# Eight weight loads of an attention and mixture-of-experts kernel, moved on SyncE's queue from batches 4 to 12 of attention into batches 12 to 15

## The reference

```python
x = x + attention(layernorm(x), ctx_512, ctx_512)
x = x + moe(layernorm(x), gate_w, w1, w2, w3)

# attention: 16 batches, 128 queries and 128 keys, 32 query heads on 8 key heads, head size 8
scores = einsum('bkgsd,bktd->bkgst', q, k) / sqrt(8)
out = einsum('bkgst,bktd->bkgsd', softmax(scores), v)

# moe: 2048 tokens of 256, 8 experts of width 512, the best 2 of each token
probs = softmax(einsum('ti,ei->te', xt, gate_w))
weights, indices = top_k(probs, 2); weights = weights / weights.sum(-1)
x1 = silu(einsum('ti,eoi->teo', xt, w1)); x3 = einsum('ti,eoi->teo', xt, w3)
out = sum over the two experts of weights * einsum('teo,eio->tei', x1 * x3, w2)
```

## Time and profile before

| | us |
|---|---|
| median of 3 timed runs | 450.33 |
| lowest, highest | 449.58, 451.56 |
| the profiled execution | 449.8 |
| its span | 448.0 |
| mean granted clock of TensorE in it | 0.92 |

### The profile page before, as it was taken

One profiled execution on the slowest core, in us unless ns is written; L12 is line 12 of the kernel. 1 busy time (PEld: TensorE's weight loads), 2 busy tenths in 40 slices (PEclk: granted clock), 3 DMA queues, 4 the chain that ended last, 5 costly groups with the idle time before them and its releaser, 6 DMA issues.

```text
span 448.0 us, 8599 instructions
## 1 busy us (share of the span) xinstructions
PE 363.3 (81%) x2234; PEld 259.2 (58%) x2256; DVE 234.7 (52%) x659; ACT 197.6 (44%) x397; POOL 183.8 (41%) x361
## 2 busy tenths in 40 slices
PE   0177988888789889873139999999999999999991
PEld 0045444455445444322127888888888888888870
DVE  6776796888678857656962332322232322232320
ACT  3325777776567646787313222223222223222220
POOL 6661363377646534576411222233222233222232
PEclk9997999999799979885559999999999999999997
DMA  6676888988977785331420333333333333333222
GB/s 197 153 150 110 228 230 200 256 192 250 221 231 169 173 243 164 107 121 50 174 72 25 51 58 49 58 48 47 48 57 48 55 51 47 47 56 50 35 23 23
DMA packets 46209, 51.16 MB, mean 114 GB/s; under 512 B 18659, under 2 KB 39267, under 8 KB 46179
## 3 DMA queue, kind: packets, MB, share of 16 engines
q1 hardware_dynamic: 37299, 39.64, 34.9%
q0 software_dynamic: 7152, 9.34, 13.2%
q10 hardware_dynamic: 1728, 1.82, 1.3%
HBM read 31.51 MB, written 16.69 MB: 108 GB/s over the span
## 4 chain that ended last, share of the span: by engine, by line
PE 58%; DMA 13%; DVE 10%; POOL 6%; issue 6%; SPq 4%; ACT 2%; POOLq 0%; ACTq 0%
PE bank L898 25%; PE bank L916 15%; DMA qst<-negT 10%; PE bank L908 4%; DVE wlo L1306 3%; PE bank L720 3%; PE bank L733 3%; PE bank L697 3%; PE bank L694 2%; PE bank L886 2%; DMA qparts_d<-qp 2%; POOL slots_d L545 2%; SPq L315 1%; SPq L282 1%; PE bank L773 1%
## 5 line engine op out<-in xcount | busy, mean ns | idle before, releaser
L660 POOL DMA_INDIRECT out_rows<-ys,meta x39 | 60.9, 1561 | 155.5 <-DVE ys L1537 149.3
L1251 DVE TENSOR_REDUCE negm<-bank 128x4 f32<-128x512 f32 x128 | 84.3, 682 | 27.6 <-PE bank L697 23.9
L1530 DVE TENSOR_TENSOR gat<-bank,sil 128x512 f32<-128x512 f32 x39 | 27.0, 692 | 112.5 <-PE bank L898 112.5
L967 ACT ACTIVATE prob<-bank 128x512 f32<-128x512 f32 x128 | 73.0, 596 | 27.4 <-PE bank L720 22.0
L916 PE MATMUL bank<-w,gT 128*128 x312 | 73.9, 380 | 0.8 <-ACT gT L1171 0.8
L1165 ACT ACTIVATE sil<-bank 128x512 f32<-128x512 f32 x39 | 23.3, 598 | 105.8 <-PE bank L898 105.8
L898 PE MATMUL bank<-whi,xhi 128*128 x156 | 60.3, 468 | 1.2 <-ACT xhi L1159 1.2
L916 PEld LDWEIGHTS bank<-w,gT 128*128 128x128 f32 x312 | 56.3, 190 | 7.1 <-issue 1.0
L697 PEld LDWEIGHTS bank<-kst,qst 125*128 125x128 bf16 x512 | 42.2, 103 | 25.0 <-issue 5.4
L720 PE MATMUL bank<-qst,kst 128*128 128x512 bf16 x107 | 43.2, 409 | 13.5 <-DMA qst<-negT 11.5
L697 PE MATMUL bank<-kst,qst 125*128 125x128 bf16 x512 | 52.6, 229 | 0.5 <-issue 0.2
(11 more groups left out here) (121 smaller groups left out, 479.3 us busy)
## 6 DMA issues: line engine op xcount, KB each, us to landing
xs<-slots_d SPq DMA_DIRECT2D x39, 129.0 KB, 2.0
w<-in_w1T SPq DMA_DIRECT2D x8, 512.0 KB
w<-in_w3T SPq DMA_DIRECT2D x8, 512.0 KB
w<-in_w2T SPq DMA_DIRECT2D x8, 512.0 KB
qparts_d<-qp SPq DMA_DIRECT2D x16, 192.0 KB, 4.4
qst<-qparts_d SPq DMA_DIRECT2D x16, 192.0 KB
qst<-qparts_d SPq DMA_DIRECT2D x16, 128.0 KB
vblk<-in_v SPq DMA_DIRECT2D x16, 128.0 KB
```

The lines of the kernel that those rows point to most:

```text
L660: pool.indirect_dma_start(out, IndirectOffsetOnAxis(ap=meta[:, r4, 0:1].bitcast(I32), axis=0), ys[:, r4, :], None, compute_op=ALU.add).the ...
L967: act.activation(prob[:, k, :], ps_e[k % 2][:, :], ACT.Exp, scale=SCALE).then_inc(exp_done, 1)
L1251: dve.tensor_reduce(negm[:, b % 2, g * G:(g + 1) * G], ps_s[(8 * b + g) % 3][:, :].rearrange("p (h t) -> p h t", h=G), AX.X, ALU.max, nega ...
L1530: dve.tensor_tensor(gat[:, u, :], ps_h3[u][:, :], sil, ALU.mult).then_inc(g_done, 1)
```

## The change

The eight calls of load_w2 on SyncE's queue move. Before, they stand in turns 4, 5, 6, 8, 8, 10, 11 and 12 of the loop; after, in turns 12, 13, 13, 14, 14, 15, 15 and 15. Nothing else is changed. The instructions of TensorE, VectorE, ScalarE and POOL are the same, in the same order.

```diff
--- before.py
+++ after.py
@@ -367,6 +367,12 @@
             load_x(12)
             load_x(15)
             for i in range(-2, B):
+                if i == 13:
+                    load_w2(1)
+                if i == 14:
+                    load_w2(3)
+                if i == 15:
+                    load_w2(5)
                 if i == 7:
                     load_w13(11)
                 if i % 2 == 0 and 2 <= i + 3 < B:
@@ -377,10 +383,6 @@
                     store_x2(i - 2)
                 if i % 2 == 1 and 0 <= i + 1 < B:
                     lay_neg(i + 1)
-                if i == 8:
-                    load_w2(3)
-                if i == 11:
-                    load_w2(6)
                 if i % 2 == 0 and 0 <= i + 1 < B:
                     lay_neg(i + 1)
                 if i % 2 == 1 and 3 <= i + 4 < B:
@@ -399,12 +401,6 @@
                     load_v(i + 1)
                 if i == 3:
                     load_w13(6)
-                if i == 4:
-                    load_w2(0)
-                if i == 5:
-                    load_w2(1)
-                if i == 8:
-                    load_w2(4)
                 if i == 2:
                     load_w13(4)
                 if i % 2 == 1 and 0 <= i + 1 < B:
@@ -417,10 +413,16 @@
                     load_w13(1)
                 if i % 2 == 0 and 8 <= i + 1 < B:
                     load_res(i + 1)
+                if i == 12:
+                    load_w2(0)
+                if i == 13:
+                    load_w2(2)
+                if i == 14:
+                    load_w2(4)
+                if i == 15:
+                    load_w2(6)
                 if i == 3:
                     load_w13(7)
-                if i == 10:
-                    load_w2(5)
                 if i % 2 == 0 and 0 <= i - 4 < B - 2:
                     copy_rows((i - 4) // 2)
                 if i % 2 == 1 and 2 <= i + 4 < B:
@@ -435,13 +437,11 @@
                     load_w13(3)
                 if i % 2 == 0 and 2 <= i + 4 < B:
                     load_k(i + 4)
-                if i == 6:
-                    load_w2(2)
                 if i % 2 == 1 and 0 <= i - 1 < B:
                     store_x2(i - 1)
                 if i == 2:
                     load_w13(5)
-                if i == 12:
+                if i == 15:
                     load_w2(7)
                 if i == 8:
                     load_w13(13)
```

## The result

Over 18 timed runs each, the kernel before took 449.94 us (median) and the changed kernel 444.74. The ratio is 0.9895, with a 95% interval of 0.9871 to 0.9919, so the change makes the kernel 1.05% faster. Forecast were 445.3 us, in a range of 440.5 to 452. The profiled execution of the changed kernel took 443.68 us, with a span of 441.8 us and a mean granted clock of 0.943, where before had 448.0 and 0.92. One profile is one execution: the timed runs of before spread from 446.1 to 454.1 us and those of after from 442.1 to 450.3, as wide as the effect. The ratios and their intervals leave out the executions that ran over 1.5% above a kernel's fastest at a lower granted clock, while a median in us is over all timed ones.

The account below looks back on a forecast made before the run. Attention's end sets when the expert tiles start, and DMA is crowded within attention. Terms -2.6 (waits), -3.3 (clock) and +0.9 (last four batches) sum to -5.0 us, from 450.33 to 445.3 us, range 440.5 to 452.

Parts of the forecast that it names:

- term A: Crowded middle of attention: TensorE's waits for lay_neg at batches 6, 8, 10 and 12 shrink, -2.6 us (0 to 5.3 gained).
- term B: Middle of attention: one of two 6.8 us stretches with TensorE's clock at 0.50 goes, -3.3 us (0 to 6.6 gained).
- What bounds the kernel: Attention's end decides when expert tiles start; in attention DMA is crowded, 0.85 busy from 80.3 to 166.1 us.
- What a load costs: Middle of attention: each 512 KB load takes all 16 engines 1.9 us; seven give back 13.6 us, share 0.85 to 0.69.
- Term C: Last four batches: moved loads delay lay_neg(15) and perhaps other small transfers, +0.9 us (0 to 3.4).
- the first: Batch 14, in Term C: lay_neg(14), with two loads ahead instead of one, still lands within its 5.67 us cover.
- The third: Batch 15, in Term C: copy_rows(5), with w2(4) in front, lands at 194.0 us, before POOL's scatter wants it at 194.92.
- The waits stay: Middle of attention: other transfers keep the queue full, lay_neg still lands in 6 us, nothing gained; 450.2 us, chance 0.24.
- Everything goes well: Whole attention stage: wait and clock gains come in full, late batches cost nothing; 440.5 us, chance 0.08.
- The slower one: Last batches decide: lay_neg(14) and (15) land in 7.32 us, TensorE waits 5.1 us, clock may fall; 452.8 us, chance 0.15.

Follow-up runs that it names:

- e11: Kernel before, its seven w2 loads still in the middle (turns 4 to 10) but each right behind a lay_neg; 449.33 us, ratio 1.007.
- e12: Kernel before, plus seven w2 pieces loaded a second time at the changed kernel's places in batches 12 to 15; 452.37 us, ratio 0.999.
- e1: Changed kernel with all eight w2 loads issued behind the last copy_rows, after batch 15; 447.93 us, ratio 0.994.
- e2: Changed kernel with w2(0), (1), (4) and (7) issued behind copy_rows(4), (5) and (6) instead of ahead; 444.62 us, ratio 0.988.
- e9: Changed kernel with the late w2 loads put where the trace of before shows the DMA engines idle; 441.94 us, ratio 0.981.
- e7: Changed kernel with lay_neg issued by ScalarE on its own DMA queue instead of by SyncE; 455.5 us, ratio 1.014.
- e3: Kernel before plus five dummy TensorE products ahead of each lay_neg wait from batch 1 on, no transfer moved; 450.12 us, ratio 1.003.
- e5: Kernel before with w2(3) to (6) moved to turns 14 and 15, the other w2 loads left in place; 451.0 us, ratio 1.003.
- e6: Kernel before with w2(0), (1), (2) moved to turns 12 and 13, the other w2 loads left in place; 446.93 us, ratio 0.997.
- e4: Changed kernel plus five dummy TensorE products ahead of each lay_neg wait from batch 1 on; 442.32 us, ratio 0.984.
- e10: e9 plus five dummy TensorE products ahead of each lay_neg wait from batch 1 on; 443.1 us, ratio 0.986.

## Why the prediction was right, and which of its steps were not

**The sum.** Forecast -5.0 us, measured -5.2 by the medians. That it came so close is in part luck: in this pair of profiles term A brought nothing and term B more than its value, and the two misses made up for each other. In the profiles the middle, batch 5 to 13, went from 85.9 to 79.9 us, -6.0, where terms A and B together said -5.9; the rest came in ahead of the first moved load (lay_neg(5) at 78.89 instead of 80.28, the same instructions, so chance) and went again in the last batches.

**What bounds the kernel.** Right. Attention sets when the tiles start, and these keep 217.2 us behind the same 13.59 us of waiting for split_lo.

**What a load costs.** Too high. Between the issues of lay_neg(5) and lay_neg(13) the busy time of the 16 engines went from 0.85 x 85.8 = 72.9 us to 0.77 x 79.87 = 61.5. That is 11.4 us for seven loads, 1.6 us each and not 1.9. The forecast share of 0.69 also left the stretch at its old length, though it was to get shorter.

**Term A, the waits (-2.6).** In this pair of profiles its step failed. Batches 6, 8, 10 and 12 waited 0, 1.70, 1.19 and 0.27 us, 3.2 instead of 5.26, which looks like -2.1. But batches 5, 9 and 13 wait more than before, and the sum over batches 5 to 13 rose from 7.7 to 9.4 us. The landings did not shrink: lay_neg(8) took 8.03 us against 7.32 in the earlier trace rows, and lay_neg(10) 6.55 against 6.46 on the chain of before. Over all profiles a smaller gain may be there: the waits of batches 5 to 13 are 7.7, 11.8 and 10.5 us in before, e11 and e12, and 9.4, 6.6, 8.3 and 8.5 in the changed kernel, e1, e2 and e9, in the mean 1.8 us less, with ranges that overlap. The reasoning from loads that stand ahead of lay_neg in SyncE's queue falls with e11 (loads behind it cost as much) and e7 (another queue lands no sooner). Shown is that batches 5 to 13 take 85.9, 86.7 and 87.4 us with seven loads in that stretch and 79.3 to 81.8 us with none and lay_neg on SyncE: 86.7 against 80.6 in the mean, 6.1 us.

**Term B, the clock (-3.3, one of two stretches).** Right in kind, too small in size, and sharper than foreseen in its place. The two stretches of 6.8 us at 0.50 are gone, and one of 3.4 us behind batch 13 has come: 10.2 us less at the lower clock, worth 5.1 us by the prediction's own way of counting. Over all profiles one place stands out, from lay_neg(8) to lay_neg(9): 14.7 to 16.1 us in all six kernels that have w2(0) to (2), or all seven loads, in turns 4 to 10, and 11.3 to 12.4 us in all eight others. Part of it is clock. From the first product of batch 8 to lay_neg(9) before took 124.73 - 117.36 = 7.4 us and after 119.83 - 115.54 = 4.3, the same work at 0.50 and at 1.00. How much of the total comes by the clock is not settled. Half of the time at 0.50 is 6.5 us in the mean of before, e11 and e12, and 0.9 in that of the four without loads, so by this count 5.6 of the 6.1 us in the middle are clock. With dummies, seven loads cost 84.0 us against the mean of 80.0 and 80.4, 3.8 us, of which e3's remaining stretch at 0.50 is 1.7; so 2.1 us are left that are not clock. In the timed runs the mean clock differs by 0.007, which over 448 us is 6.3 us at the lower level, or 3.1 us of the 5.2. These three estimates put the clock at 0.6 to 0.9 of the gain, where the forecast had 3.3 of 5.9. Against them stand e3's timed runs, which reached the changed kernel's clock and won nothing, as far as the dummies' own time doesn't hide a gain.

**Term C, the last four batches (+0.9).** The size fits the profile of the changed kernel (65.9 us instead of 64.8, +1.1) and lies between the nothing and the 2 us that e12 and the other profiles leave; the timed runs of e12 can neither confirm nor exclude it. Of its steps the first held: lay_neg(14) was covered, and lay_neg(15), issued at 178.84, cost TensorE 0.35 us. The third was called harmless and was the one that counted: copy_rows(5) was forecast to land in 4.8 us, ahead of the scatter that wanted it. It took 4.42 at the least, until POOL's own work was done, and its scatter came 1.6 us late, which fits a later landing, though the trace names no cause for that wait. copy_rows(4), which I had not costed, took 6.24 us, but made its scatter only 0.3 us late. I had taken the scatter's place in the profile of before as its due time; counted from the copy's issue, POOL's own work ended 5.1 us behind it before (194.10 + 0.22 against 189.24) and 4.4 us in the changed kernel.

**The rivals.** "The waits stay" was right about the waits and wrong about the time. "Everything goes well" had -11.9 us; three quarters of its clock part came (5.1 of 6.6), its waits did not. The slower one did not come: lay_neg(15), issued at 178.84, let TensorE go on at 182.10, 3.3 us later and not 7.3.

**What stays open.** By which wait the traffic of the middle costs the part that is not clock isn't settled. The waits for lay_neg don't show it in this pair. VectorE's waits for TensorE's scores fell from 11.5 to 8.7 us and ScalarE's for the exp products from 13.0 to 9.1, but these are waits for TensorE itself. Open too is why batch 8, and nothing else, splits so cleanly. Its waits for lay_neg are 1.98 to 3.31 us in the six kernels and at most 1.70 in the eight, but a wait of 2.28 us at batch 5 of the changed kernel had no low clock behind it, so length alone does not decide. Batch 13's wait of 2.29 us in the changed kernel did have one behind it, and that of 3.36 us in e9 had none. And the halves of e5 and e6 don't add: four loads fewer in the middle won nothing in e5, so the cost is not in proportion to the traffic.

## What to carry to other kernels

Weights that are wanted only in the next stage belong where the DMA engines are idle, not merely where their order is free: the same 4 MB cost 1% in the crowded middle, wherever they stood in the issue order there, at most 2 us in the last four batches, too little for the timed runs to tell from nothing, and 4.3 us where they met the next stage's own first transfers. Read the granted clock of TensorE over the same stretch in each profile before a length is put down to transfers: here it may have carried more than half of the difference. Look for the place by the DMA share in short windows, and check from both sides which small transfer has work waiting for it, those just ahead of the load as well as those just behind. Where one execution differs from the next by as much as the effect, take the same stretch out of many profiles before a single wait is believed.

## What the runs showed of the hardware

A transfer of 24 KB took 5.0 to 8.5 us to land while the DMA engines were 0.69 to 1.03 busy, from SyncE's queue (5.02 at 0.85, 6.21 at 0.69, 8.03 at 0.96) and from ScalarE's own (6.81 at 0.78, 8.46 at 1.03), and at most 2.7 us where they fell idle behind it. copy_rows(4), 256 KB inside the on-chip memory, took 3.0, 4.3, 6.0 and 6.1 us where one w2 load followed it (before, e11, e3, e5), 3.9 us with none near (e1), and 5.0 to 6.5 us with two, one ahead and one behind (after, e4, e12) or both behind (e2, e9, e10). So a second load is not what decides it alone. The row of before:

```profile
rows<-rows SPq DMA_DIRECT2D x1, 256.0 KB, 3.0
```

With dummy products ahead of the waits TensorE's mean clock went from 0.933 to 0.941 (e3) and from 0.940 to 0.949 (e4). In e3 that paid nothing, as the dummies take time themselves; e4 was 0.5% faster than the changed kernel, with intervals that meet.
